# A sandwich layer's closing slots: v's low products last, a later first weighted sum in every fourth slot, and the first two tiles' output projection begun earlier and in another bank

## What is computed

```python
x = x + layernorm(attention(layernorm(x)) @ Wo)       # q, k rotated; causal; softmax(q k / 8) v
router = einsum('bsd,hd->bsh', n, Wr) + br            # n = layernorm(x)
scores = H * softmax(router)
low = einsum('bsd,hrd->bshr', n, A)
x = x + layernorm(2 * einsum('bshr,hor,bsh->bso', low, B, scores))
```

## Time and profile before

| | |
|---|---|
| median of 3 runs | 1071.71 us (1071.65 to 1073.65) |
| the profiled execution | 1071.34 us |
| its span, first to last instruction | 1069.5 us |
| PE busy | 1038.8 us, 97% |
| DVE busy | 751.4 us, 70% |
| ACT busy | 623.4 us, 58% |
| POOL busy | 420.0 us, 39% |
| mean granted TensorE clock | 0.998 |

### The profile page before, as it was taken

How to read it: one execution, slowest core, us unless ns; L and a number is a source line. 1 busy time by engine, 2 the same in 40 slices (tenths; PEclk the granted TensorE clock), 3 DMA queues, 4 the chain that set the end, 5 groups by cost and what they waited for, 6 DMA issues and landing times.

```text
span 1069.5 us, 19431 instructions
## 1 busy us (share of the span) xinstructions
PE 1038.8 (97%) x6135; PEld 896.2 (84%) x6135; DVE 751.4 (70%) x2170; ACT 623.4 (58%) x1454; POOL 420.0 (39%) x422
## 2 busy tenths in 40 slices
PE   7999999999999999999999999999989999999996
PEld 6987888788888888888888888888867888888884
DVE  8576777677766667666666767676666877777777
ACT  7566667666666666656665656656676333334324
POOL 5142524352452536244442624353467332333221
PEclk9999999999999999999999999999999999999999
DMA  7013323331221236111111101110243323322311
GB/s 295 21 65 109 109 70 109 109 109 51 89 67 39 88 136 239 57 51 50 53 41 62 50 16 50 50 51 11 64 165 89 97 91 115 118 90 89 115 60 60
DMA packets 58701, 90.84 MB, mean 85 GB/s; under 512 B 3569, under 2 KB 36337, under 8 KB 58609
## 3 DMA queue, kind: packets, MB, share of 16 engines
q1 hardware_dynamic: 58464, 89.44, 26.0%
q10 hardware_dynamic: 144, 0.26, 0.1%
HBM read 64.52 MB, written 25.17 MB: 84 GB/s over the span
## 4 chain that ended last, share of the span: by engine, by line
PE 81%; DVE 6%; ACT 4%; issue 4%; POOL 3%; DVEq 0%; ACTq 0%; POOLq 0%
PE bank L1519 28%; PE bank L1464 23%; PE bank L1544 14%; PE bank L1576 5%; PE bank L1596 3%; PE bank L1595 2%; PE bank L1714 2%; POOL wv_lo L672 2%; PE bank L1691 1%; DVE q_hl L1149 1%; DVE prob L1117 1%; ACT prob L801 1%; POOL prob L649 1%; PE bank L1715 1%; ACT q_hl L822 1%
## 5 line engine op out<-in xcount | busy, mean ns | idle before, releaser
L649 POOL TENSOR_SCALAR prob<-prob,rinv 128x128 f32<-128x128 f32 (+3 forms) x256 | 137.1, 536 | 456.3 <-DVE rinv L1127 456.0
L801 ACT ACTIVATE prob<-prob,nmax 128x128 f32<-128x128 f32 (+3 forms) x256 | 144.3, 564 | 244.6 <-DVE nmax L1117 242.3
L1519 PE MATMUL bank<-big_hi,w_hi 128*128 128x512 f32 (+1 forms) x520 | 217.0, 417 | 0.3 <-DVE big_lo L1092 0.3
L1519 PE MATMUL bank<-big_hi,w_lo 128*128 128x512 f32 (+1 forms) x520 | 203.2, 391 | 0.0
L1519 PE MATMUL bank<-big_lo,w_hi 128*128 128x512 f32 (+1 forms) x520 | 202.2, 389 | 0.0
L1117 DVE CUSTOM_DVE_ANT_0 prob<-bank,mask 128x256 f32<-128x256 f32 (+2 forms) x192 | 106.3, 554 | 70.5 <-PE bank L1464 70.1
L1544 PE MATMUL bank<-wv_hi,big_hi 128*128 128x256 f32 x512 | 132.6, 293 | 0.0
L1544 PE MATMUL bank<-wv_hi,big_lo 128*128 128x256 f32 x512 | 127.3, 282 | 0.0
L1135 DVE TENSOR_TENSOR pT<-bank,pT 128x128 fp32r<-128x128 f32 (+3 forms) x256 | 124.2, 485 | 1.6 <-ACT pT L812 1.3
L1576 PE MATMUL bank<-ident,prob 128*128 128x128 f32 x640 | 111.8, 272 | 4.4 <-DVE pT L1135 2.5
L1519 PEld LDWEIGHTS bank<-big_hi,w_lo 128*128 128x128 f32 x520 | 97.6, 188 | 21.6
(11 more groups left out here) (159 smaller groups left out, 2243.6 us busy)
## 6 DMA issues: line engine op xcount, KB each, us to landing
w_raw<-in_wqkv SPq DMA_DIRECT2D x32, 512.0 KB, 4.5
wv_raw<-in_wqkv SPq DMA_DIRECT2D x16, 512.0 KB, 4.5
attention_out<-o_sum SPq DMA_DIRECT2D x64, 128.0 KB, 2.3
w_raw<-attention_out SPq DMA_DIRECT2D x16, 512.0 KB, 4.8
land<-in_x SPq DMA_DIRECT2D x16, 512.0 KB, 3.7
out<-res SPq DMA_DIRECT2D x14, 512.0 KB, 2.7
xin<-in_x SPq DMA_DIRECT2D x12, 512.0 KB, 4.0
xT_hold_hi<-xin SPq DMA_DIRECT2D x8, 512.0 KB, 3.6
```

Of the source, the lines that this page charges most:

```text
L649: pool.tensor_scalar(p, p, rinv[:, q % 4:q % 4 + 1], 1.0, ALU.mult, ALU.mult).then_inc(prob_done, 1)
L801: act.activation(prob[:, q % 4, 0:n], prob[:, q % 4, 0:n], ACT.Exp, scale=-1.0, bias=nmax[:, q % 4:q % 4 + 1], accum_out=rsum[:, q % 4:q % ...
L1519: done = pe.matmul(grp_ps[k][:, cols], w, xt[:, cols], start=at == 0, stop=at == GROUP_MM - 1)
```

## The change

1. `v_project` does all 32 products with `wv_hi`, for both row tiles, and then the 16 with `wv_lo`. The bank is opened by a start flag on the very first product alone.
2. In slots with u % 4 == 3 the first weighted sum, `o_lower` and `o_add` stand one step later (`first_sum_at`): sum in step 1, the other two in step 2.
3. `Y_FIRST` begins in step 6 of slot 31 and ends in step 5 of slot 32; `Y_SECOND` goes from step 6 of slot 32 to step 2 of slot 33 and does the first half of tile 1 and four products of the second. What is left behind the slots is four products instead of eight.
4. Tile 1's first half goes to v's bank (`y_bank`), and `x2_turn` of tile 0's first half to bank 2. The waits follow.
5. `oT_low(1, 1)` moves from steps 4 and 5 to 3 and 4 of slot 32; `y_variance(0, 0)` from step 1 of slot 33 to step 7 of slot 32; tile 0's scaling and sums from step 3 to step 2 of slot 33; the two `ln_start` from steps 2 and 4 to 0 and 3, the second ahead of the last `o_lower`.

```diff
@@ -50,11 +50,13 @@
 CHUNKS = 8
-Y_FIRST = (((0, 0), (0, 1), (0, 2)), ((0, 3), (0, 4)), ((1, 0), (1, 1)), ((1, 2), (1, 3)), ((1, 4), (0, 5)),
-           ((1, 5),), ((0, 6), (1, 6)), ((0, 7), (1, 7)))
-Y_SECOND = ((0, 1), (2, 3, 4), (5, 6, 7))
+Y_FIRST = (((0, 0), (0, 1)), ((0, 2), (0, 3)),
+           ((1, 0), (1, 1), (1, 2)), ((1, 3), (1, 4)), ((0, 4), (0, 5)), ((1, 5), (0, 6)), ((1, 6),), ((0, 7), (1, 7)))
+Y_SECOND = (((0, 0), (0, 1)), ((0, 2), (0, 3)), ((0, 4), (0, 5)), ((0, 6), (0, 7), (1, 0)), ((1, 1), (1, 2), (1, 3)))
 WO_EARLY = UPH - 2
 WO_SLOT = STEPS * (UNITS - 2)
+Y_FIRST_AT = STEPS * UNITS - 2
+Y_SECOND_AT = Y_FIRST_AT + len(Y_FIRST)
 WO_AT = {STEPS * WO_EARLY + 4: 0} | {WO_SLOT + s: c for s, c in ((4, 1), (9, 2), (10, 3), (12, 4), (13, 5), (16, 6), (17, 7))}
@@ -326,6 +328,10 @@
+        def first_sum_at(u):
+            return 1 if u % QUAD == QUAD - 1 else 0
         def v_job(m):
@@ -420,9 +426,13 @@
-            if isinstance(t, int) and t == 0 and k == 1:
-                return pt_ps[0]
+            if isinstance(t, int) and t == 0:
+                return pt_ps[0] if k == 1 else sc_ps[0]
             return grp_ps[0] if final(t) and k == 1 else tr_ps
+        def y_bank(t, i, k):
+            return tr_ps if isinstance(t, int) and t == 1 and k == 0 else y_ps[i][k]
@@ -692,8 +702,8 @@
                         oT_low(0, 0)
-                    if isinstance(u, int) and u == UNITS and s in (4, 5):
-                        oT_low(1, 1, PART * (s - 4), PART * (s - 3))
+                    if isinstance(u, int) and u == UNITS and s in (3, 4):
+                        oT_low(1, 1, PART * (s - 3), PART * (s - 2))
                     if isinstance(u, int) and u == UNITS + 1 and s == 2:
@@ -870,7 +880,7 @@
                     pt_high(u, s)
-                    if s == 1 and real(u - 2):
+                    if s == 1 + first_sum_at(u) and real(u - 2):
                         o_lower(u - 2, 0)
@@ -902,14 +912,13 @@
                             oT_high(2, 0, 32)
-                        if s == 2:
+                        if s == 0:
                             ln_start(ln_first(0))
...
                             act.activation(ar_hi, ar_raw[:, :, :], ACT.Copy).then_inc(ffn_hi_done, 1)
+                            ln_start(ln_second(0))
                             o_lower(u - 2, 1)
-                        if s == 4:
-                            ln_start(ln_second(0))
                     if isinstance(u, int) and u == UNITS and s == 5:
@@ -1221,18 +1230,19 @@
                         hold_chunk(u, HOLD_AT.index(s), half, ahead)
+                    if u == UNITS and s == 7:
+                        y_variance(0, 0)
                     if isinstance(u, int) and u == UNITS + 1:
-                        if s == 1:
-                            y_variance(0, 0)
-                        if s == 3:
-                            dve.memset(br_sb[:, 0:HR], 0.0).then_inc(br_zeroed, 1)
-                            dve.memset(ones[:, :], 1.0).then_inc(ones_set, 1)
+                        if s == 2:
                             y_scale(0, 0)
...
                             ln_variance(ln_second(0))
+                        if s == 3:
+                            dve.memset(br_sb[:, 0:HR], 0.0).then_inc(br_zeroed, 1)
+                            dve.memset(ones[:, :], 1.0).then_inc(ones_set, 1)
                             o_add(u - 2, 1)
@@ -1251,7 +1261,7 @@
                         dve.wait_ge(res_done, t - 1)
-                dve.scalar_tensor_tensor(out=x1_of(t, i)[:, half(k)], in0=y_ps[i][k][:, :], scalar=rs1[:, 0:1],
+                dve.scalar_tensor_tensor(out=x1_of(t, i)[:, half(k)], in0=y_bank(t, i, k)[:, :], scalar=rs1[:, 0:1],
                                          in1=xres[:, i, half(k)], op0=ALU.mult, op1=ALU.add
@@ -1412,7 +1422,7 @@
             dve.wait_ge(y0_done, 1)
-            half_stats(0, y_ps[1][0][:, :])
+            half_stats(0, y_bank(1, 1, 0)[:, :])
             for t in range(2, 6):
@@ -1524,8 +1534,10 @@
                 for mm in range(2 * first, 2 * (first + count)):
-                    t, at = mm // GROUP_MM, mm % GROUP_MM
-                    c, part = (at // 2, at % 2) if at < 2 * KC else (at - 2 * KC, 2)
+                    if mm < 4 * KC:
+                        t, c, part = mm // (2 * KC), mm % (2 * KC) // 2, mm % 2
+                    else:
+                        t, c, part = (mm - 4 * KC) // KC, mm % KC, 2
                     if mm == 0:
@@ -1534,7 +1546,7 @@
                             pe.wait_ge(tr_lo, kept)
-                    if mm == 2 * KC:
+                    if mm == 4 * KC:
                         pe.wait_ge(wv_lo_done, 2 * g + 2)
@@ -1542,7 +1554,7 @@
                     done = pe.matmul(v_bank(m)[:, 2 * P * t:2 * P * t + 2 * P].rearrange("p (a n) -> p a n", a=2), x_t, w,
-                                     start=at == 0, stop=at == GROUP_MM - 1)
+                                     start=mm == 0, stop=mm == 2 * GROUP_MM - 1)
                 if first + count == GROUP_MM:
@@ -1602,13 +1614,16 @@
                     if isinstance(t, int) and t == 0:
-                        pe.wait_ge(rot_done, 2 * UNITS)
+                        pe.wait_ge(rot_done, 2 * UNITS - 1)
                     pe.wait_ge(oT_hi_done, t + 1)
...
                     if isinstance(t, int) and t == 1:
-                        pe.wait_ge(neg_done, STEPS * UNITS - 1)
+                        pe.wait_ge(v_hi_done, 2 * UNITS)
+                        pe.wait_ge(v_lo_done, 2 * UNITS)
                     if late(t, 2):
                         pe.wait_ge(x1_done, t - 1)
+                if isinstance(t, int) and t == 0 and k == 1 and c0 == 0:
+                    pe.wait_ge(rot_done, 2 * UNITS)
                 if isinstance(t, int) and t == 1 and k == 1 and c0 == 0:
@@ -1616,7 +1631,7 @@
                     cols = slice(512 * k, 512 * k + 512)
-                    last = products(y_ps[i][k][:, :], [(oT_hi[:, i, c, :], wo_hi[c][:, cols]),
+                    last = products(y_bank(t, i, k)[:, :], [(oT_hi[:, i, c, :], wo_hi[c][:, cols]),
                                                        (oT_lo[:, i, c, :], wo_hi[c][:, cols]),
@@ -1646,7 +1661,7 @@
                     project_next(per * s + 2 * third, per - 2 * third)
-                    if s == 0:
+                    if s == first_sum_at(u):
                         attend(u - 2, b, 0)
@@ -1655,12 +1670,12 @@
-                    if isinstance(u, int) and STEPS * u + s in range(STEPS * UNITS, STEPS * UNITS + len(Y_FIRST)):
-                        for k, c in Y_FIRST[STEPS * (u - UNITS) + s]:
+                    if STEPS * u + s in range(Y_FIRST_AT, Y_SECOND_AT):
+                        for k, c in Y_FIRST[STEPS * u + s - Y_FIRST_AT]:
                             y_half(0, 0, k, c, c + 1)
-                    if isinstance(u, int) and u == UNITS + 1 and s < len(Y_SECOND):
-                        for c in Y_SECOND[s]:
-                            y_half(1, 1, 0, c, c + 1)
+                    if STEPS * u + s in range(Y_SECOND_AT, Y_SECOND_AT + len(Y_SECOND)):
+                        for k, c in Y_SECOND[STEPS * u + s - Y_SECOND_AT]:
+                            y_half(1, 1, k, c, c + 1)
@@ -1678,8 +1693,7 @@
                 if isinstance(t, int) and t == 0 and k == 0:
-                    pe.wait_ge(v_hi_done, 2 * UNITS)
-                    pe.wait_ge(v_lo_done, 2 * UNITS)
+                    pe.wait_ge(neg_done, STEPS * UNITS)
                 elif isinstance(t, int) and t == 0:
@@ -1772,12 +1786,12 @@
-            y_half(1, 1, 1, 0, 4)
+            y_half(1, 1, 1, 4, 6)
             x2_turn(0, 0, 0)
-            y_half(1, 1, 1, 4, 6)
+            y_half(1, 1, 1, 6, 7)
             columns()
             x2_turn(0, 0, 1)
-            y_half(1, 1, 1, 6, KC)
+            y_half(1, 1, 1, 7, KC)
             for t in range(2, 6):
```

## The result

| | kernel before | changed kernel |
|---|---|---|
| median | 1072.46 us (1071.65 to 1073.65, 4 runs) | 1063.12 us (1062.93 to 1063.47, 4 runs) |
| ratio, with its 95% interval | | 0.9912 [0.9895, 0.993] |
| profiled execution, its span | 1071.34, 1069.5 | 1062.93, 1061.0 |
| PE busy | 97% | 98% |
| mean granted TensorE clock | 0.998 | 0.996 |

Faster by 0.9%; the forecast of 1062.9 is met within 0.2 us. The runs of the kernel before lie in two groups some 2 us apart (10 of 15 beside the first experiments at 1071.12 to 1071.95 with a granted clock of 0.997 or 0.998, five at 1073.4 to 1073.99 with 0.995), and as all its rows come from one execution of the lower group, sums are made between spans: 1069.5 - 1061.0 = 8.5.

The account below looks back on a forecast made before the run. TensorE, busy 97%, was taken as the bound, so only its waits could be gained. Savings of 12.2 less 1.4 given back, rounded to 10.7, and 1.9 lost in the closing gave 1062.9 us; range 1057 to 1067.

Parts of the forecast that it names:

- Low products last, 6.2: v's projection: all seven PE waits for wv_lo go with no work added, 6.2 us less.
- Sum a step later, 6.0: Slots 3, 7, ..., 31: the first weighted sum no longer waits for v's low part, 6.0 us less.
- The margin of 0.3 us in slot 3: Slot 3, later weighted sum: PE would come at 95.9, the operand be there at 95.6.
- the slower rival: Copy and addition don't fit step 2, the exponent behind wv_hi comes late in eight slots: 18.6 us lost, 1080; chance 0.04.
- Given back in slots 3 and 7, 1.4: Slots 3 and 7: PE waits about 0.5 for w_lo and 0.2 for pT_lo, 0.7 us a slot off the gain.
- The row named: POOL's w_lo for the next projection, from 115.19 for 2.4 us: PE would wait about 0.5 us for it.
- the early slots give back more: Rival: DVE and ACT bound slots 2 to 9, waits return at transposes or w_lo, 3.3 us less gained, 1066; chance 0.12.
- The six others: The fourth slots other than 3 and 7: the chain has about 0.5 us to spare, so nothing was taken off there.
- The closing, +1.9: Slots 31 to 33: filled PE waits outweighed by a later last negation and POOL's chain to the columns, 1.9 us more.
- 1.4 for this order: Closing: if POOL's last sum starts ahead of DVE's ar_lo, the columns come at 832.0 and the closing costs 1.4 us.
- The closing pays as well: Rival: DVE does y_variance in a gap, nothing behind it moves, filled waits of 3.9 us are kept, 1057; chance 0.22.
- the filled waits (3.9): Closing: PE's waits filled with output products, 2.6 us at 796, 0.8 at 807 and 0.5 of small ones.

Follow-up runs that it names:

- slots_only: The kernel before with the new order of v's products and the later weighted sums, but the old closing: 1061.43 us, ratio 0.99.
- The last three runs: slots_w_lo_wait, stats_w_lo_wait and v_high_first, all with PE's wait for w_lo at a group's third matmul: 1061.26, 1061.58 and 1061.17 us.
- both_moves: The changed kernel with the edits of stats_later and sums_first together: 1061.69 us, ratio 0.99.
- sums_first: The changed kernel with POOL's three sums of ar ahead of bt_lo instead of behind it: 1063.13 us, ratio 0.9917.
- v_low_last: The kernel before with only the low products of v put last: 1068.77 us, ratio 0.9967.
- sum_later: The kernel before with only the first weighted sum a step later in every fourth slot: 1065.74 us, ratio 0.9942.
- slots_w_lo_wait: slots_only with PE's wait for w_lo moved to the third matmul of a group, the first that reads it: 1061.26 us, ratio 0.9891.
- v_high_first: slots_w_lo_wait with ACT copying v's high parts ahead of w_hi in slots 3 and 7: 1061.17 us, ratio 0.9896.
- closing_only: The kernel before with only the new closing, keeping the old order of v's products and weighted sums: 1074.64 us, ratio 1.002.
- stats_later: The changed kernel with y_variance(0, 0) back in slot 33, step 1, and its ln_start in step 2: 1061.51 us, ratio 0.9898.
- stats_w_lo_wait: stats_later with PE's wait for w_lo moved to the third matmul of a group, the first that reads it: 1061.58 us, ratio 0.9894.

## Why the prediction came out right, point by point

- **Low products last, 6.2.** The seven waits went. In the five later slots the step is right: 3.4 forecast (6.2 less the two longest, 1.4 each), 3.5 measured. In slots 3 and 7 it was worth 2.8 by the waits, and gave 0.8 on top of part 2 (0.46 and 0.35 at slots 5 and 9). Alone it would have given as much (1.48 - 0.68), had the halved clock not taken 1.48.
- **Sum a step later, 6.0.** Alone it gave 6.0 by the medians, 5.5 by the traces. The margin of 0.3 us in slot 3 held (95.70, no wait), and the exponent behind wv_hi was not late (in slot 19 it still waits 0.35 for its negation, 0.60 before): the slower rival is out.
- **Given back in slots 3 and 7, 1.4.** This term was too small. The waits there were worth 2.8 + 4.3 = 7.1, and slots_only gained 2.36 + 2.14 = 4.5 in them: 2.6 given back. The row named was a right one: w_lo, 0.38 us at 115.59 and 0.39 at 215.88. But I took it as the only price on that path, with 0.2 for pT_lo, and its chain (w_lo, w_sum, w_hi, v, k_low under the lock, pT_lo) holds the slot at three more places, all ahead of turns (the transposes of the probabilities): from slot 3's last steps to slot 4's end PE of slots_only falls back by 0.36, 0.38 (w_lo), 0.33 and 0.31 us against before, and by about as much four slots on. The last three runs free the second of these and then the transposes behind it, and each time the next place takes it back. This is the rival "the early slots give back more" in a milder form.
- **The six others.** Five gave 5.2 instead of 4.7. Slot 31 gave its 0.5 (slots_only is 10.5 us ahead in its middle), but the closing behind it let only 0.1 of that through.
- **The closing, +1.9.** Measured 1.5 between slot 29 and wlow, 1.6 against slots_only. The order of the steps was right, and all the following is against slots_only: wo_lo 0.70 and 0.61 (forecast 0.85 and 0.7 to 0.85), oT_low 0.54 (0.7), last negation 1.5 later (2.0), oT_high(2, 0) 2.0 later (2.45), and POOL's ar_sum went ahead of DVE's ar_lo and took 0.47 instead of the 1.61 of the earlier trace rows, so that the columns came only 0.8 us late. From there on the step failed: I had the loss end at the columns, 1.4 for this order. The stand itself halves PE's clock, 1.48 us that the forecast didn't know, of which DVE's wlow hides 0.9. The size came out right with another make-up: that is luck.
- **"The closing pays as well".** Refuted: the filled waits (3.9) turn up as PE's stand of 2.24 before the columns, and with the statistics put back still as 1.50 there and 0.53 at wlow. The chain that ends the closing runs over the last negation, the exponent, oT_high(2, 0) and POOL. Nothing that PE did earlier here shortened it, and the 1.3 us that PE lost in slots_only didn't lengthen it.

In sum, by the traces: 0.26 (start-up) + 4.5 + 5.2 - 1.5 = 8.5, forecast 8.8. The start-up is chance. Parts 1 and 2 brought 9.8 instead of 10.7, and the closing cost 1.6 against slots_only instead of 1.9, so part of the closeness is errors that cancel; the mechanisms of parts 1 and 2, and that the closing costs, are borne out.

On the lock: that DVE's k_low and ar_lo, with two SBUF inputs, and POOL's subtractions and sums, which read SBUF, exclude each other for whole instructions is what the Trainium skill says in SBUF — State Buffer, on the shared port pair. The traces agree: 2.89 us against 0.69 for k_low, and 1.61 against 0.47 for POOL's last sum. On the clock: the Trainium skill, TensorE: Matmul & The Clock Gate, Part 1, has the two levels and a monitor whose phase is not tied to the program, so that the moment of a switch varies. The stands below, of which like lengths end either way, agree with that; no run here shows the monitor itself.

## What to carry to other kernels

A wait of the bounding engine is worth its length only where the engine that it waited for has time left in that slot: follow the freed time two or three releasers on, through the queue of the slowest helper, before you count it. Filling gaps of TensorE in a closing stage pays nothing while a chain over the other engines ends it, and work put ahead of that chain's last link cost nearly its full length (1.73 us of statistics, 1.6 at the end). A stand of TensorE may cost more behind it: 1.48 us of PE's time after one of 1.93 and after one of 2.24. And compare single executions from a common instruction on: their starts differed by up to 0.6 us here, more than some of the effects.

## What the runs showed of the hardware

Whether a stand of PE costs the clock is not told by its length alone. In the profiles above, the clock fell to 0.50 behind stands of 1.55 (both_moves), 1.69 (sums_first), 1.93 (v_low_last, slot 3), 2.17 or 2.18 (slot 31 of sum_later, slots_only, slots_w_lo_wait and v_high_first), 2.24 (changed kernel) and 2.25 us (closing_only), each time for some 3 us, in sums_first for nearly 7. It stayed at 1.00 behind 1.50 (stats_later and stats_w_lo_wait), 1.65 (sum_later, twice), 1.92 (closing_only, slot 3), 1.93 (slot 7 of before, closing_only and v_low_last), 2.00 (before, slot 3) and 2.32 (slot 31 of before and v_low_last). The same kernel, v_low_last, has a stand of 1.93 in slot 3 with a fall and one of 1.93 in slot 7 without. The fall doesn't come with the stand's end either: in slots_only and sums_first PE worked for 1 us at full clock first, in both_moves for 2. What decides was not settled.

The same kernel's runs 1.3 to 2 us apart (before, closing_only, sums_first) go with the clock: every run of before at 1073.4 or above, in all the experiments, has a granted clock of 0.995 or 0.996, every one below 1072 has 0.997 or 0.998. So the upper runs spend more of their time at half clock, and 1.48 us is what one such fall cost PE above. Where in the kernel it falls in them is not shown, for no profile of an upper run of before was taken.
